# One-pass transpositions for residuals and U, U's sums on eviction, and new engine orders in a MetaFormer block

## The chip, the cores and the metric

One Trainium2 chip, one of its cores. The time is the device time in microseconds of one launch of the whole program; the kernel before has a median of 410.23 us over 3 runs (408.69 to 413.77).

## The reference

The input `x` is (8, 64, 32, 32), all float32. Four blocks follow one another, each with a residual:

```
x = x + conv0(ln_c(x))    # q, k, v by 1x1 products; softmax(k) over the 1024 pixels, softmax(q) over 16 channels
                          # of each of 8 heads; context = k v^T (16x16); out = q context; Wout, bout
t = tokens(x)             # (8, 1024, 64)
t = t + ffn0(ln_t(t))     # routing per IMAGE: mean over tokens @ Wr, softmax, capacity scale, top 2 of 8 experts;
                          # 64 -> 128 gelu -> 64 by the two experts; layer norm with gamma, beta
x = x + conv1(ln_c(x))    # 3x3 convolution 64 -> 64 with weights scaling * sign(W)
t = t + ffn1(ln_t(t))     # routing per TOKEN: softmax of logits, top 2 of 8; all 8 experts computed, weighted, summed
```

## The kernel before, in words

Everything stays in SBUF. There are two parts.

**Part one, attention**, goes over 4 pairs of images (two images of 64 channels fill 128 partitions). XC holds the pair in channels by pixels. `centre` turns tiles of 128 pixels into tokens with the channel mean subtracted (a product with the matrix `cen`), ScalarE squares, VectorE sums, GpSimd (POOL) takes the power -0.5, VectorE normalises, `xn_to_channels` turns back, `keys_values` (L530) gives keys and values. The context chain is `key_max`, `key_exp`, `kv_to_tokens` (L537), `tokens_kv`, `context` (L544), `pick_context` (Z), `context_turned` (L549), `block_diagonal` (BD), `context_out` (L559, L561), `outputs` (M). The queries go in 4 units per pair, each 2 tiles of pixels of 2 images: `queries` (L577), `query_max`, `query_exp`, `query_sum`, `qnorm` (POOL), `q_to_channels` (L589), `query_channels`. The residual of a unit opens a PSUM bank: `residual` (L605) multiplies a tile of XC by `ic`, a constant of 256 columns that holds for each image the identity and the centring matrix beside each other, so the bank gets the pixels as tokens and the centred tokens; `attend` (L618) accumulates the attention's output onto both. ScalarE squares the centred part and copies the other into T (L1267, L1270), VectorE and POOL make the token norm, `normalise2` writes U. `u_to_channels` (L632) multiplies U by IDS, an identity with a column of ones, which gives U in channels and, in column 129, its sum over the tile's tokens; `u_channels` (ScalarE, L1279) copies both into UT. After pair 3 the router (L1002 and on) sums those columns and picks two experts for each image.

**Part two** goes image by image, software pipelined: while image b goes through its 8 experts (`f_hidden` L696, `f_gelu` L1388, `f_gated` L1186, `f_output` L801), image b+1 goes through the convolution and the token router (`a_vT`, `b_conv`, `b_to_tokens`, `b_residual`, `b_centre`, `b_ss`, `b_normalise`, `b_to_channels` L759, `b_gates` L766, `b_logits`, `b_probs`, `b_first`, `b_second`, `b_weights`, `b_gates_turned` L772) and image b+2 through the image-routed layer (`a_hidden`, `a_output` L712, `a_z_turned`, `a_sum`, `a_ss0`, `a_zn`, `a_residual`, `a_centre`, `a_ss1`, `a_normalise`). The 8 x 1024 token weights GT are stored to DRAM and loaded back, each broadcast to 128 partitions (GB, 512 KB each); `f_gated` multiplies by them. The outputs of the 8 experts accumulate in a PSUM bank; `f_start` adds the weighted biases (B2X times GT, L789) and the residual (TF times the identity, L791) with `start=False` between `f_output2` and `f_output3`, in program order behind `b_gates` of the next image. `f_result` copies the bank out, which is stored.

Each engine runs one stream. The order in it is written out by hand: `ATTENTION_PLAN` for part one and `PLAN` for part two give, per engine, a cyclic list of parts; `name+2` in period p is that part for pair or image p+2. Parts named `set_` run once (where p + ahead is 0) and prepare weights: `set_conv` (L863 to L873) makes the signs of the convolution weights in place in W1stage, loaded last by the sync engine's queue, writes WC, and sums the absolute weights from a second load into W1stage that waits for the signs. A queue never looks past a waiting instruction; dependencies between engines are counting semaphores.

## Time and profile before

| | us |
|---|---|
| median of 3 runs | 410.23 |
| the profiled execution, its own time | 412.51 |
| its span, first to last instruction | 410.7 |
| TensorE busy | 344.7 (84%) |
| VectorE, ScalarE, POOL busy | 278.7, 230.0, 92.8 |
| DMA moved | 41.17 MB |

The profile is one execution. Part one runs to about 118 us, the router to 127, a start-up of part two with little overlap to about 180, six full image periods to about 357, and the last image to the end. A float32 product is two MATMUL records, a transposition one. Records of TensorE overlap in time, so what a part costs is read from its start to the next start. The granted clock of TensorE (PEclk) is 1 at 2.4 GHz and 0.5 at 1.2 GHz; a share between them is a stretch with both.

### The profile page before, as it was taken

What the parts mean: (1) busy time and instruction counts of PE and PEld (TensorE: products, weight loads), DVE (VectorE), ACT (ScalarE), POOL (GpSimd) and SP (SyncE); (2) the same over time, 40 slices, a digit from 0 to 9 for tenths busy, and PEclk for the clock granted to TensorE, in tenths of its full rate; (3) what the DMA queues carried; (4) which work ended last, traced back from release to release, by engine and by line L of the source; (5) the groups of instructions that cost most, each with busy time, mean ns of one, the idle gap of its engine ahead of it and who ended that gap; (6) DMA issues with size and microseconds to landing.
All of it is one profiled execution on the core that took longest, in us unless ns stands there. A gap on an engine that the chain in (4) does not pass through costs nothing.

```text
span 410.7 us, 5254 instructions
## 1 busy us (share of the span) xinstructions
PE 344.7 (84%) x1751; PEld 188.1 (46%) x1751; DVE 278.7 (68%) x587; ACT 230.0 (56%) x392; POOL 92.8 (23%) x77
## 2 busy tenths in 40 slices
PE   4879899998927146689999999999999999888975
PEld 4357687876922032333443443443443444344222
DVE  3486995959441524727977968868959959966662
ACT  2445466464525314555756857857857856736631
POOL 5226271643410111211112112103103103102000
PEclk9699999999975758579999999999999999999988
DMA  6941000000000000028039048057066065073092
GB/s 153 178 119 31 1 2 2 0 2 1 2 1 0 0 2 1 0 74 339 1 103 336 0 128 311 0 155 285 0 207 233 0 229 211 3 292 144 26 344 95
DMA packets 25835, 41.17 MB, mean 100 GB/s; under 512 B 15376, under 2 KB 16144, under 8 KB 25808
## 3 DMA queue, kind: packets, MB, share of 16 engines
q1 hardware_dynamic: 25808, 40.83, 30.9%
q8 instruction: 14, 0.23, 0.2%
q14 instruction: 13, 0.11, 0.1%
HBM read 38.47 MB, written 2.36 MB: 99 GB/s over the span
## 4 chain that ended last, share of the span: by engine, by line
PE 41%; DVE 25%; issue 13%; ACT 10%; POOL 5%; DMA 3%; POOLq 1%; ACTq 0%; SPq 0%; DVEq 0%
PE ps L696 9%; PE ps L742 6%; PE ps L801 5%; POOL rstdA L457 4%; PE ps L605 3%; PE ps L712 3%; DVE HB L1186 3%; PE ps L618 2%; PE ps L530 2%; PE ps L513 2%; PE ps L727 2%; DVE qsum L964 2%; ACT XC L1336 2%; ACT HB L1388 2%; DVE ssA L1092 2%
## 5 line engine op out<-in xcount | busy, mean ns | idle before, releaser
L696 PE MATMUL ps<-ET,W1B 64*128 64x512 f32 x256 | 70.4, 655 | 6.9 <-ACT HB L1388 5.3
L1186 DVE TENSOR_TENSOR HB<-HB,GB 128x1024 f32<-128x1024 f32 x44 | 53.1, 1220 | 23.9 <-DMA GB<-spread 23.8
L1388 ACT ACTIVATE HB<-ps,B1B 128x1024 f32<-128x1024 f32 x44 | 47.8, 1111 | 9.4 <-PE ps L696 5.3
L457 POOL TENSOR_TENSOR rstdA<-varA,pow_half 128x8 f32<-128x8 f32 x16 | 28.8, 1801 | 90.8 <-DVE varA L886 90.8
L801 PE MATMUL ps<-HB,W2B 128*64 128x512 f32 x176 | 45.2, 617 | 3.7 <-DVE HB L1186 3.7
L457 POOL TENSOR_TENSOR rstdB<-varB,pow_half 128x8 f32<-128x8 f32 x8 | 14.0, 1750 | 124.7 <-DVE varB L886 124.7
L696 PEld LDWEIGHTS ps<-ET,W1B 64*128 64x128 f32 x256 | 21.9, 194 | 35.8 <-issue 12.0
L457 POOL TENSOR_TENSOR rstd<-var,pow_half 128x4 f32<-128x4 f32 (+1 forms) x24 | 29.0, 1217 | 21.1 <-DVE var L886 20.8
L742 PE MATMUL ps<-VP,WC 128*128 128x512 f32 x96 | 28.4, 450 | 1.4 <-ACT VP L1356 1.4
L1186 DVE TENSOR_TENSOR XC<-XC,GB 128x1024 f32<-128x1024 f32 x20 | 24.2, 1219 | 5.9 <-DMA GB<-spread 5.9
L472 POOL TENSOR_TENSOR QS<-QS,rqsum 128x512 f32<-128x512 f32 x16 | 16.9, 1057 | 44.1 <-DVE rqsum L967 44.1
L742 PEld LDWEIGHTS ps<-VP,WC 128*128 128x128 f32 x96 | 19.3, 208 | 11.9 <-ACT VP L1356 6.6
L801 PEld LDWEIGHTS ps<-HB,W2B 128*64 128x64 f32 x176 | 11.1, 137 | 27.5 <-issue 23.6
L1388 ACT ACTIVATE XC<-ps,B1B 128x1024 f32<-128x1024 f32 x20 | 21.7, 1109 | 3.5 <-PE ps L801 2.1
L1356 ACT ACTIVATE VP<-ps 128x512 fp32r<-128x512 f32 x16 | 9.8, 612 | 23.2 <-PE ps L727 23.2
L696 PE MATMUL ps<-UT,W1S 64*128 64x512 f32 x64 | 20.4, 721 | 2.6 <-ACT B1S L1327 2.6
L801 PE MATMUL ps<-XC,W2B 128*64 128x512 f32 x80 | 21.4, 622 | 0.0
L1336 ACT ACTIVATE XC<-ps,B1S 128x1024 f32<-128x1024 f32 x16 | 17.8, 1112 | 2.8 <-PE ps L696 2.8
L1363 ACT ACTIVATE CV<-ps,CSCALE 128x512 f32<-128x512 f32 x8 | 5.5, 687 | 23.6 <-PE ps L742 23.6
L727 PE MATMUL ps<-ident_r,US 128*128 128x128 f32 x64 | 9.0, 267 | 11.5 <-DVE US L1082 9.9
L712 PE MATMUL ps<-XC,W2S 128*64 128x512 f32 x64 | 17.3, 629 | 1.3 <-ACT XC L1336 1.3
L1257 ACT ACTIVATE QT<-ps 128x512 f32<-128x512 f32 x16 | 9.8, 610 | 14.9 <-PE ps L589 14.9
(214 smaller groups left out, 666.7 us busy)
## 6 DMA issues: line engine op xcount, KB each, us to landing
GB<-spread SPq DMA_DIRECT2D x64, 512.0 KB, 7.9
out<-W1stage SPq DMA_DIRECT2D x8, 256.0 KB, 3.4
XC<-in_x SPq DMA_DIRECT2D x6, 256.0 KB, 5.7
...
```

The source lines that it names most:

```text
L457: pool.tensor_tensor(out_, var, pow_half[:, 0:n], ALU.pow).then_inc(s[rstd_sem], 1)
L472: pool.tensor_tensor(q, q, rqsum[:, n % 2, :].unsqueeze(2).broadcast_to([P, 32, KD]), ALU.mult)\
L605: ins = mm(a[:, j * 256:(j + 1) * 256], XC[:, p, t * P:(t + 1) * P], ic, start=(j == 0), stop=False, skip_group_check=True)
L696: mm(ps[:, H_BANKS[n % 2][c], :], weights[half(c), :], tokens(half(c)), start=True, stop=True).then_inc(s["h"], 1)
L712: ins = mm(ps[c * C:(c + 1) * C, A_BANK, :], W2S[:, k, :], HA[:, k, c * HALF:(c + 1) * HALF], start=(k == 0), stop=(k == 1), skip_group_ch ...
L727: ins = pe.transpose(ps[:, A_BANK, j * P:(j + 1) * P].bitcast(F32R), VS[:, 2 * j + h].rearrange("p k c -> p (k c)"), ident_r[:, :])
L742: ins = mm(ps[:, B_BANK, :], WC[:, dx, 3 - r:5 - r, :].rearrange("p k c -> p (k c)"), VP[:, par, r:r + H - 1:2, dx:dx + W], start=(r == 0 ...
L801: ins = mm(acc(b)[c * C:(c + 1) * C, :], W2B[:, e, :], HG[b][e][:, c * HALF:(c + 1) * HALF], start=(e == 0), stop=(e == E - 1), skip_group ...
L1186: tt(HG[b][e], HG[b][e], GB[:, e, :], ALU.mult).then_inc(s["f_hg"], 1)
L1257: av(QT[:, n % 2].rearrange("p r n -> p (r n)"), ps[:, QT_BANK, :], ACT.Copy).then_inc(s["qT"], 1)
L1336: av(HA[:, k, :], HID[n % 2], ACT.Gelu, bias=B1S[:, k:k + 1]).then_inc(s["gelu"], 1)
L1388: av(HG[b][e], HID[n % 2], ACT.Gelu, bias=B1B[:, e:e + 1]).then_inc(s["gelu"], 1)
```

## The change

- `residual` opens the bank with two transpositions (`is_transpose=True`, identity) and two products with `cen`, in place of two products with the 256 columns of `ic`.
- `u_to_channels` transposes; the sums over tokens come from `accum_out` of ScalarE's evictions, which are now one per image (USUM). IDS, its memset and its copy are gone.
- `f_start` becomes four transpositions of TF that open the accumulation ahead of `f_output0`; the bias products are a part of their own, `f_bias`, and `b_gates_out` waits for that.
- The lists of both plans are new, on all engines.

```diff
     vec=(
-        "query_sum2-2 query_max3-2 sum_squares1_1-1 normalise1_0-1 sum_squares2_0-2 query_sum3-2 normalise1_1-1 "
...
+        "sum_squares2_0-2 set_bo-1 query_sum3-2 normalise2_0-2 key_max-1 query_max0-1 sum_squares2_1-2 "
...
-                        ins = mm(a[:, j * 256:(j + 1) * 256], XC[:, p, t * P:(t + 1) * P], ic, start=(j == 0), stop=False,
+                        both = a[:, j * 256:(j + 1) * 256].rearrange("p (i x c) -> p i x c", i=2, x=2)
+                        mm(both[:, :, 0, :], XC[:, p, t * P:(t + 1) * P], ident, start=(j == 0), stop=False,
+                           is_transpose=True, skip_group_check=True)
+                        ins = mm(both[:, :, 1, :], XC[:, p, t * P:(t + 1) * P], cen, start=False, stop=False,
                                  skip_group_check=True)
...
-                        ins = mm(ps[:, UT_BANK, i * (P + 1):(i + 1) * (P + 1)],
-                                 U[:, 2 * p + i, UT_ * g:UT_ * g + UT_, :].rearrange("p h c -> p (h c)"), IDS[:, :],
-                                 start=True, stop=True)
+                        ins = pe.transpose(ps[:, UT_BANK, i * P:(i + 1) * P],
+                                           U[:, 2 * p + i, UT_ * g:UT_ * g + UT_, :].rearrange("p h c -> p (h c)"), ident)
...
             def f_start(b, par):
 
+                pe.wait_ge(s["b_t"], b + 1)
+                ge(pe, s["f_out"], b - 1)
                 for j in range(4):
-                    mm(acc(b)[:, j * P:(j + 1) * P], B2X[:, j, :], GT[:, par, :], start=False, stop=False,
-                       skip_group_check=True)
                     ins = mm(acc(b)[:, j * P:(j + 1) * P], TF[:, par, j].rearrange("p h c -> p (h c)"), ident,
-                             start=False, stop=False, skip_group_check=True)
+                             start=(j == 0), stop=False, is_transpose=True, skip_group_check=True)
                 ins.then_inc(s["f_start"], 1)
+
+            def f_bias(b, par):
+
+                pe.wait_ge(s["b_cwt"], b + 1)
+                for j in range(4):
+                    ins = mm(acc(b)[:, j * P:(j + 1) * P], B2X[:, j, :], GT[:, par, :], start=False, stop=False,
+                             skip_group_check=True)
+                ins.then_inc(s["f_bias"], 1)
...
-                    src = ps[:, UT_BANK, 0:2 * (P + 1)].rearrange("p (b n) -> p b n", b=2)
-                    av(UT[:, 2 * p:2 * p + 2, g, :], src, ACT.Copy).then_inc(s["uT"], 1)
+                    for i in range(2):
+                        ins = av(UT[:, 2 * p + i, g, :], ps[:, UT_BANK, i * P:(i + 1) * P], ACT.Identity,
+                                 accum_out=USUM[:, 2 * p + i, g:g + 1])
+                    ins.then_inc(s["uT"], 1)
```

**VectorE in part one, between pairs 0 and 1.** Before: block_diagonal and `query_max2` of pair 0, then `sum_squares1_0` of pair 1 (L904 with L886), and so on; `set_conv` (L863, L866) comes 17 rows behind the first L904.

```order
L940 TENSOR_TENSOR BD<-ps,K 128x128 x2
L951 TENSOR_REDUCE qmax<-ps 128x32
L955 TENSOR_TENSOR QS<-ps,qmax 128x512
L904 TENSOR_REDUCE ss<-SQ 128x8
L886 TENSOR_SCALAR var<-ss 128x8
L964 TENSOR_REDUCE qsum<-QS 128x32
L967 RECIPROCAL rqsum<-qsum 128x32
L951 TENSOR_REDUCE qmax<-ps 128x32
L955 TENSOR_TENSOR QS<-ps,qmax 128x512
```

Now (lines are moved by the change; L868 to L878 are `set_conv`, L909 is `sum_squares1`):

```order
L945 TENSOR_TENSOR BD<-ps,K 128x128 x2
L956 TENSOR_REDUCE qmax<-ps 128x32
L960 TENSOR_TENSOR QS<-ps,qmax 128x512
L868 TENSOR_SCALAR W1stage<-W1stage 128x576
L871 TENSOR_SCALAR WC<-W1stage 128x3x192
L876 TENSOR_REDUCE CSCALE<-W1stage 128x1
L878 TENSOR_SCALAR CSCALE<-CSCALE 128x1
L909 TENSOR_REDUCE ss<-SQ 128x8
L891 TENSOR_SCALAR var<-ss 128x8
L909 TENSOR_REDUCE ss<-SQ 128x8
L891 TENSOR_SCALAR var<-ss 128x8
```

`set_conv` with its two loads now stands ahead of the sums of squares of pair 1.

**TensorE in part two, an image period,** from `f_output7` on: before, then now (L696 `f_hidden`, L801 and now L807 `f_output`, L759 `b_to_channels`, L766 `b_gates`, L789 and L791 `f_start`; now L791 `f_start`, L799 `f_bias`).

```order
L801 MATMUL ps<-XC,W2B 64x512 x2
L719 MATMUL ps<-K,QS 128x128 x4
L696 MATMUL ps<-ET,W1B 128x512 x4
L801 MATMUL ps<-HB,W2B 64x512 x6
L759 MATMUL ps<-K,QS 128x128 x4
L696 MATMUL ps<-ET,W1B 128x512 x2
L766 MATMUL ps<-GW,ET 128x16 x4
L789 MATMUL ps<-GT,B2X 128x128
L791 MATMUL ps<-K,QT 128x128
```

```order
L807 MATMUL ps<-HB,W2B 64x512 x2
L719 MATMUL ps<-K,QS 128x128 x4
L807 MATMUL ps<-XC,W2B 64x512 x2
L696 MATMUL ps<-ET,W1B 128x512 x2
L807 MATMUL ps<-XC,W2B 64x512 x2
L696 MATMUL ps<-ET,W1B 128x512 x4
L759 MATMUL ps<-K,QS 128x128 x4
L799 MATMUL ps<-GT,B2X 128x128 x4
L766 MATMUL ps<-GW,ET 128x16 x4
L791 MATMUL ps<-K,QT 128x128 x4
L807 MATMUL ps<-HB,W2B 64x512 x2
L696 MATMUL ps<-ET,W1B 128x512 x4
```

Two `f_output` parts moved between the hidden parts, the bias products ahead of `b_gates`, `f_output2` behind `f_start`.

**TensorE, the last image,** from its `f_hidden5` before, and from `f_output5` of the image before on now.

```order
L696 MATMUL ps<-ET,W1B 128x512 x4
L801 MATMUL ps<-HB,W2B 64x512 x4
L801 MATMUL ps<-XC,W2B 64x512 x2
L696 MATMUL ps<-ET,W1B 128x512 x2
L789 MATMUL ps<-GT,B2X 128x128
```

```order
L807 MATMUL ps<-HB,W2B 64x512 x6
L696 MATMUL ps<-ET,W1B 128x512 x2
L807 MATMUL ps<-HB,W2B 64x512 x2
L696 MATMUL ps<-ET,W1B 128x512 x4
L799 MATMUL ps<-GT,B2X 128x128 x4
L807 MATMUL ps<-XC,W2B 64x512 x4
L807 MATMUL ps<-HB,W2B 64x512 x8
```

`f_hidden5` to `f_hidden7` stand behind `f_output0` now (the last two of each eight hidden products behind `f_output1`), and only the bias products are left between the outputs.

## Rows read from the trace of the kernel before

**Rows 1.** Stages by windows; per engine busy us (instructions), then clock, DMA, GB/s.
```profile
51.20:75.40 24.20, 22.55 (x155) 18.39 (x156) 18.54 (x42) 14.26 (x35) 11.44 (x11) 1.00 0.01 1
...
250.00:275.00 25.00, 24.25 (x120) 10.74 (x117) 21.09 (x43) 18.03 (x27) 5.29 (x3) 1.00 0.33 110
```

**Rows 2.** TensorE's timeline, a pair: start, us, engine, line, what [idle before, releaser].
```profile
85.53 1.93 PE L530 MATMUL ps<-XN,WKV 128*64 128x512 f32 x4 [0.36 <-ACT XN L1216]
...
89.69 0.60 PE L589 MATMUL ps<-K,QS 128*128 128x128 f32 x4
90.13 0.61 PE L632 MATMUL ps<-IDS,U 128*128 128x129 f32 x4
90.58 1.03 PE L577 MATMUL ps<-WQB,XN 128*128 128x256 f32 x4
91.44 1.03 PE L605 MATMUL ps<-K,XC 128*128 128x256 f32 x4
92.30 1.03 PE L577 MATMUL ps<-WQB,XN 128*128 128x256 f32 x4
...
98.48 0.40 PE L549 MATMUL ps<-K,Z 32*128 32x32 f32 x2 [0.69 <-DVE Z L934]
```

**Rows 3.** Timelines: keys_values of pairs 1 and 2; the router's first operation.
```profile
36.86 1.93 PE L530 MATMUL ps<-XN,WKV 128*64 128x512 f32 x4 [0.20 <-ACT XN L1216]
...
61.34 1.07 PE L530 MATMUL ps<-XN,WKV 128*64 128x512 f32 x2 [0.36 <-ACT XN L1216]
...
117.39 0.21 DVE L1002 TENSOR_REDUCE u<-UT 128x8 f32<-128x32 f32 x1 [1.27 <-ACT UT L1279]
```

**Rows 4.** TensorE's timeline, one image of the second part.
```profile
259.21 0.47 PE L789 MATMUL ps<-GT,B2X 128*128 128x128 f32 x2
...
261.17 1.99 PE L696 MATMUL ps<-ET,W1B 64*128 64x512 f32 x8
...
265.74 1.13 PE L696 MATMUL ps<-ET,W1B 64*128 64x512 f32 x4 [0.71 <-ACT HB L1388]
...
279.35 1.08 PE L712 MATMUL ps<-XC,W2S 128*64 128x512 f32 x4 [0.22 <-ACT XC L1336]
```

**Rows 5.** VectorE's timeline, then tile W1stage's view with its DMAs.
```profile
29.35 0.69 DVE L904 TENSOR_REDUCE ss<-SQ 128x8 f32<-128x512 f32 x1 [0.62 <-ACT SQ L1205]
...
37.20 0.75 DVE L866 TENSOR_SCALAR WC<-W1stage 128x576 fp32r<-128x576 f32 x1
40.97 0.75 DVE L871 TENSOR_REDUCE CSCALE<-W1stage 128x1 f32<-128x576 f32 x1 [3.01 <-DMA W1stage<-in_wcs]
...
L426 SPq DMA_DIRECT2D W1stage<-in_wconv x1: 444/444/444, 26.8 to 26.8; - x1
...
DMA to landing us min/median/max: 2.8/2.9/3.0
```

**Rows 6.** Windows, as in rows 1, behind two stretches with little TensorE work.
```profile
394.10:399.00 4.90, 4.88 (x14) 1.23 (x16) 4.29 (x4) 1.11 (x1) 0.00 (x0) 0.65 1.02 380
...
164.60:172.00 7.40, 6.69 (x20) 3.68 (x20) 4.80 (x12) 2.95 (x5) 1.46 (x1) 0.50 0.00 0
```

**Rows 7.** TensorE's timeline, the last image.
```profile
389.25 1.99 PE L696 MATMUL ps<-ET,W1B 64*128 64x512 f32 x8
394.12 3.17 PE L801 MATMUL ps<-HB,W2B 128*64 128x512 f32 x8 [2.88 <-DVE HB L1186]
...
402.56 3.60 PE L801 MATMUL ps<-HB,W2B 128*64 128x512 f32 x16
```

**Rows 8.** ScalarE's timeline in a pair.
```profile
92.28 0.18 ACT L1231 ACTIVATION_READ_ACCUMULATOR KV<-KV,nkmax 32x1 f32 x1
92.37 0.36 ACT L1279 ACTIVATE UT<-ps 128x258 f32<-128x258 f32 x1
```

**Rows 9.** VectorE's and ScalarE's timelines, the same image as rows 4.
```profile
258.68 1.22 DVE L1186 TENSOR_TENSOR HB<-HB,GB 128x1024 f32<-128x1024 f32 x1
...
262.63 0.63 ACT L1348 ACTIVATE XN<-XNT 128x512 f32<-128x512 f32 x1 [1.22 <-DVE XNT L1110]
```

More of the change, by code:

```diff
@@ L117 @@
     pool=(
[L118 removed]
+        "qnorm3-2 rstd2_1-2 qnorm0-1 rstd2_2-2 qnorm1-1 rstd2_3-2 rstd1_0 rstd1_1 qnorm2-1 rstd2_0-1"
     ).split(),
     pe=(
[L121 to L123 removed]
@@ L124 @@
-        "keys_values0+2 keys_values1+2 residual2+1 u_to_channels3 attend2+1 q_to_channels3+1 u_to_channels0+1 "
-        "queries0+2 residual3+1 queries1+2"
+        "queries2+1 kv_to_tokens+1 residual3 u_to_channels0 context+1 attend3 context_turned+1 q_to_channels0+1 "
+        "u_to_channels1 context_out+1 centre0+2 set_outputs+2 centre1+2 residual0+1 set_fold+2 queries3+1 "
+        "q_to_channels1+1 attend0+1 residual1+1 u_to_channels2 xn_to_channels0+2 attend1+1 xn_to_channels1+2 "
+        "keys_values0+2 keys_values1+2 q_to_channels2+1 set_second-2 queries0+2 queries1+2 residual2+1 "
@@ L126 @@
+        "q_to_channels3+1 u_to_channels3 attend2+1"
     ).split(),
     vec=(
[L128 to L131 removed]
@@ L132 @@
-        "normalise2_3-2"
+        "sum_squares2_0-2 set_bo-1 query_sum3-2 normalise2_0-2 key_max-1 query_max0-1 sum_squares2_1-2 "
+        "query_max1-1 normalise2_1-2 query_sum0-1 set_layer1-2 sum_squares2_2-2 order_rows1 key_norm-1 "
+        "pick_context-1 query_sum1-1 block_diagonal-1 sum_squares2_3-2 set_fold+2 normalise2_2-2 query_max2-1 "
+        "order_rows0+2 set_conv-1 sum_squares1_0 normalise2_3-2 sum_squares1_1 normalise1_0 query_sum2-1 "
+        "normalise1_1 query_max3-1"
     ).split(),
@@ L373, in build @@
             "b_eT", "b_et", "b_gate", "b_lg", "b_exp", "b_top", "b_cwT", "b_cwt", "b_out",
-            "h", "gelu", "f_hg", "f_start", "f_w2", "f_out", "f_stored",
+            "h", "gelu", "f_hg", "f_start", "f_bias", "f_w2", "f_out", "f_stored",
         ) + tuple(f"spread{e}" for e in range(E))}
```

58 lines of the change are left out of this document (23 added, 35 removed), and 8 rows, old and new, of the table pe.

## The prediction, made before the changed kernel ran

> **What bounds the kernel now.** I read the granted clock and the busy time by stage first, then TensorE's timeline in one attention pair and in one image of the second part, then the other engines at the places where TensorE waits, and last the input DMAs and the end of the run. The stage view [rows 1] shows TensorE busy for 22.55 of 24.20 us in an attention pair and for 24.25 of 25 us in the second part, at the full clock; VectorE is at 77% and 84%. So TensorE is the bound in both stages, but with waits in it. In a pair they stand at the chain over the key context, as 0.69 before `context_turned`, where VectorE's queue is late with Z [rows 2]. Summing the parts of one pair by their start-to-start times gives 21.2 us of work in a period of 24.48 and 24.19 us (`keys_values` at 36.86, 61.34 and 85.53, [rows 2, 3]): 3 us are waits. In the second part the period is 29.9 us, with two waits, 0.71 and 0.22 [rows 4].
>
> **Attention, the work.** A tile's transposition costs 0.11 us (four in 0.44, 89.69 to 90.13), an `u_to_channels` part 0.45 (to 90.58) with two float32 products, a residual part 0.86 (91.44 to 92.30) with two of 256 columns [rows 2]. Now the U part is two transpositions, 0.22. The residual part is two transpositions and two products of 128 columns, which cost what a product with the 129 columns of IDS costs, so 2 x 0.11 + 2 x 0.22 = 0.66. The gain is 0.20 + 0.23 per unit, 1.7 us per pair, and 21.2 becomes 19.5. A transposition inside an accumulation is in no row: its price lies between 0.11 and the 0.22 of the product that it replaces (residual part then 0.88, no gain); I take 0.11, since the existing ones stand between float32 products without a gap. On top of the rows: the Trainium skill's page "TensorE: Matmul & The Clock Gate", section "Terms", says that transpose mode is 4x faster for float32; these rows show 0.22 against 0.11, twice. By 4x a U part would cost 0.11 and the sum would be 1.8 us lower (16 parts).
>
> **Attention, the order.** In the new order `queries2`, `kv_to_tokens`, `residual3`, `u_to_channels0`, `context`, `attend3` and so on stand between the links of the context chain, and VectorE makes `pick_context` ahead of `query_sum1`. Laying the 30 parts of a pair out by their row durations, with each engine in its new order, leaves some 1.4 us of waits (0.6 before `context`, 0.3 and 0.4 at the two turns, the rest small). 19.5 + 1.5 = 21.0 us per pair. Bounds: 22.7 (old waits stay, or VectorE's 18.5 us of work couples badly) and 19.5. Pairs 1 to 2 and 2 to 3: 24.48 + 24.19 - 42.0 = **-6.7** (bounds -2 and -9).
>
> **Attention, the stall.** `set_conv` now stands on VectorE before `sum_squares1_0` of pair 1. It needs wconv, issued at 26.8 and landed 2.8 later, 29.6 [rows 5]; then two operations, 0.75 the longer, 1.2 together; then the second load into the same buffer, which waits for them: 3.01 us of idle before (that wait stood where VectorE would have waited for the keys anyway); then 0.75 + 0.15. So `sum_squares1_0` cannot start before about 34.9, against 29.35 [rows 5]. Behind it stand its second half (0.8 each), POOL's rstd, the normalisation and two groups of transpositions: `keys_values` of pair 1 starts at about 40.3, not 36.86 [rows 3]. That time hangs on a DMA, so the small changes at the start (WOUT's product between the halves of `centre`, under 1 us) are hidden by it. TensorE has work until about 34 and then nothing for some 4 us. After an idle stretch of 2.88 us near the end the granted clock was 0.65 over the next 4.9 us [rows 6, 7], so I count on the 1.2 GHz level for a few us here: +2.0 (bounds 0 and 4). Pair 1 is then late by **+5.5** (3.45 + 2.0; bounds +2.5 and +7.5, the low one if VectorE gets back what it no longer loses at 37 to 41).
>
> **Attention, the end.** From `keys_values` of pair 3 to the router's first operation it took 117.39 - 85.53 = 31.9 [rows 3]. The parts in it lose 2 us of work and about 1 us of waits: **-2.9** (bounds -1.5, -4). Against it ScalarE: one eviction per unit becomes two with a sum, and each sum brings a read of 0.18; the one eviction of 258 columns took 0.36 [rows 8]. Two of half its size with their reads lie between 0.72 (time goes with the columns) and 1.08 together (it doesn't); I take 0.8. ScalarE is busy 14.3 of 24.2 [rows 1], so this is hidden, except for the last unit, whose sum the router waits for: **+0.25** (bounds 0 and +1).
>
> **The second part, per image.** `f_start` was eight float32 products, 259.21 to 261.17, 1.96 us [rows 4]. Now four transpositions (0.5) and, as `f_bias`, four products (0.95): -0.45. `f_output0` and `f_output1` between `f_hidden` parts break two runs of equal products, +0.1 each. The wait of 0.71 before `f_hidden2` ends with ScalarE's gelu; ahead of that stand a table load and the squaring that waited 1.22 for VectorE's centring [rows 4, 9]. On VectorE `f_gated4` (1.22 us, at 258.68, [rows 9]) stood between `a_zn` and `a_residual`; now it fills the wait for POOL's rstd, in which `f_gated3` stood, and centring comes about 1.1 us earlier. TensorE arrives earlier too, so 0.3 to 0.4 of the wait remains. The 0.22 goes, since `f_gelu4` no longer stands behind `b_scale`. Per period -0.45 + 0.2 - 0.35 - 0.22 = -0.8 to -0.9: six of them **-5.3** (bounds -0.25 and -1.2 each). Fewer things wait for POOL or SP: both get the same instructions in the same sequence there. Before image 0, `a_residual` no longer stands behind `b_logits`: **-0.7**; in the last period **-0.6**.
>
> **The end.** `f_hidden5` and `f_hidden6` of the last image were done at 389.25 to 391.2, before the gates arrived; now they are queued behind `f_output0`, which waits for `f_gated0` and so for the GB load. From `f_output0` at 394.12 to the end at 406.16 TensorE is busy throughout [rows 7]. That stretch gains 1.9 of hidden parts and 0.2 for broken runs and loses 1.05 (`f_start` is done before, only `f_bias` stays): +1.05; and TensorE is idle from 389.3 on instead of 391.2, so the half level covers more of it: +1. **+2.1** (bounds 0 and +3.5).
>
> **Sum.** -6.7 + 5.5 - 2.9 + 0.25 - 5.3 - 0.7 - 0.6 + 2.1 = -8.35 on the profiled execution's 412.51 us, which is 2.3 above the median of 410.23; the change is the same for both, so **402.0 us**, -2.0%.
>
> **Rivals.**
> 1. *The stall costs little.* If TensorE's other parts fill it or the clock stays up, pair 1 is late by 2.5 only and the pairs come to 20.5: -12.5, **398 us**. For: the full clock held from 30 on with small waits. Against: the order leaves nothing that doesn't need VectorE.
> 2. *VectorE and its latencies set the pair.* Its 18.5 us of work per pair are as much as TensorE's 19.5; if the pairs keep their 3 us of waits, they gain 1.6 each instead of 3.3, and the end of the attention 1.5: -3.5, **406.5 us**. The same time comes out where transpositions in an accumulation are no faster than the product. For: the wait of 0.69 ended on VectorE [rows 2]. Against: the hand layout.
> 3. *Slower: the clock doesn't come back after the stall.* The place is TensorE from about 38 us on: from 164.6 on, after a wait, the granted clock was 0.50 for the whole of 7.4 us, with TensorE busy for 6.69 of them [rows 6]; 1.2 GHz is its lower level. Each us at the lower level costs 0.5; beyond about 16 us of it more than I have counted, the whole gain is gone. If it lasts through one more pair (26 us) it is +13: **415 us**. Against: attention parts are denser than those at 164, and the clock was full over whole pairs [rows 1]. The Trainium skill's page on TensorE, in its part on the transpose mode, says that the full clock does not engage for transposes, which do not count as busy in the same way; that rule speaks against this change. By it the 48 transpositions of a pair, 5.3 of 19.5 us, would not count; before it was 32 of them, 3.5 of 21.2 us, and the clock was full, so the trace gives it little weight.
>
> **Chances.** Forecast 0.50 (its own range 400 to 405), rival 1 0.24, rival 2 0.20, rival 3 0.06. The range, 395.5 to 408, takes in rivals 1 and 2 with most of the bounds. 2% is about what a measurement of this kernel can tell from no change: under 402.0 is half of the forecast and all of rival 1, 0.49; over 418.4 is the worst half of rival 3, 0.03; the rest, 0.48, lies within 2%.
>
> **What would show it.** VectorE's wait before the reduction of WCS stays near 3 us and moves to about 31 to 34, and `sum_squares1_0` of pair 1 starts at 34 to 35; the clock drops shortly after. `keys_values` start near 42, 63.5 and 84.5; the router's first operation near 113.5. The U transpositions come at 0.11 us each. The image period is 29.0 with one wait of 0.3 to 0.4 before `f_hidden2`. At the end some 14 us pass from `f_output0` of the last image to the last product. It is wrong if the transpositions among products are slower than 0.11, if an image period stays above 29.5 with new waits, or if pair 1 is not late.

## The result, and the profile after

The changed kernel takes 393.72 us (median of 4 runs, 393.04 to 394.83) against 411.08 (408.69 to 413.77) of the kernel before on the same chip: ratio 0.958, 95% interval 0.951 to 0.965. The forecast was 402.0 in a range of 395.5 to 408: the sign was right, and the gain is twice the one forecast. The profiled execution took 394.83, its span went from 410.7 to 393.0.

From the page of the changed kernel: span, busy time per engine, then TensorE's busy share and granted clock in 40 slices.

```profile
span 393.0 us, 5235 instructions
PE 333.8 (85%) x1719; PEld 179.1 (46%) x1719; DVE 279.6 (71%) x586; ACT 233.6 (59%) x440; POOL 93.0 (24%) x76
PE   3868999999817155889999999999999999898695
PEclk9978999999966658599999999999999999999968
```

TensorE is busy for 10.9 us less (344.7 before), ScalarE for 3.6 more (230.0 before, the sums on eviction are its work), VectorE and POOL for the same within 1 us. I cut both spans at the same parts:

| stretch | before | after | difference | forecast |
|---|---|---|---|---|
| start to `keys_values`, pair 1 | 36.86 | 40.47 | +3.6 | +5.5 |
| pairs 1 to 2 and 2 to 3 | 48.67 | 40.77 | -7.9 | -6.7 |
| pair 3 to the router's first operation | 31.86 | 28.67 | -3.2 | -2.65 |
| router to `f_hidden2` of image 0 | 56.89 | 56.03 | -0.9 | -0.7 |
| six periods, `f_hidden2` of image 0 to 6 | 181.16 | 171.26 | -9.9 | -5.3 |
| last period | 27.66 | 26.99 | -0.7 | -0.6 |
| `f_hidden2` to `f_output0`, last image | 11.02 | 9.94 | -1.1 | 0 |
| `f_output0` to the end of the span | 16.6 | 18.9 | +2.3 | +2.1 |

They add up to -17.7. Half of the error is in the image periods. Of the six periods before, the first took 31.66 and the others 29.90 each; now the first takes 28.18, four take 28.49 and the last 29.13.

TensorE's timeline of the changed kernel (start, us, what, idle before); these rows answer to [rows 2, 3], the router's to the last of rows 3:

```profile
40.47 2.01 PE L530 MATMUL ps<-XN,WKV 128*64 128x512 f32 x4
...
60.86 2.01 PE L530 MATMUL ps<-XN,WKV 128*64 128x512 f32 x4
...
81.24 2.01 PE L530 MATMUL ps<-XN,WKV 128*64 128x512 f32 x4
```
```profile
109.91 0.19 DVE L1007 TENSOR_REDUCE u<-USUM 128x8 f32<-128x32 f32 x1 [1.20 <-ACT UT L1284]
```

A transposition that opens an accumulation, and the product behind it, in a residual part; all of these starts are 0.11 and 0.22 apart, so the part costs 0.66 as I took it:

```profile
35.83 0.27 PE L606 MATMUL ps<-K,XC 128*128 128x128 f32 x1
35.94 0.39 PE L608 MATMUL ps<-K,XC 128*128 128x128 f32 x2
36.16 0.27 PE L606 MATMUL ps<-K,XC 128*128 128x128 f32 x1
36.27 0.39 PE L608 MATMUL ps<-K,XC 128*128 128x128 f32 x2
```

Windows over one pair and one image period of the changed kernel, which answer to [rows 1]:

```profile
60.86:81.24 20.38, 20.25 (x156) 16.85 (x156) 18.62 (x42) 15.01 (x47) 11.49 (x10) 1.00 0.01 2
251.09:279.58 28.49, 28.31 (x134) 12.04 (x134) 23.95 (x47) 20.74 (x31) 5.29 (x4) 1.00 0.45 158
```

TensorE is busy for all but 0.13 of a pair and 0.18 of an image period, at the full clock. Before, 24.19 held 22.55 of busy time, and an image period of 29.90 held 28.93. So its busy time fell by 2.3 per pair and by 0.62 per image, and its idle time by 1.5 per pair (1.64 to 0.13) and 0.8 per image. One image period, with the waits of [rows 4]: 0.71 has become 0.18, and before the two halves of L712, which now run as one, nothing is left of 0.22.

```profile
251.09 1.13 PE L696 MATMUL ps<-ET,W1B 64*128 64x512 f32 x4 [0.18 <-ACT HB L1395]
...
263.40 1.94 PE L712 MATMUL ps<-XC,W2S 128*64 128x512 f32 x8
```

VectorE ahead of pair 1, which answers to [rows 5]: the stall is where it was forecast, with the length that it was forecast to have.

```profile
30.35 0.75 DVE L871 TENSOR_SCALAR WC<-W1stage 128x576 fp32r<-128x576 f32 x1
34.05 0.75 DVE L876 TENSOR_REDUCE CSCALE<-W1stage 128x1 f32<-128x576 f32 x1 [2.95 <-DMA W1stage<-in_wcs]
34.84 0.15 DVE L878 TENSOR_SCALAR CSCALE<-CSCALE 128x1 f32<-128x1 f32 x1
34.91 0.68 DVE L909 TENSOR_REDUCE ss<-SQ 128x8 f32<-128x512 f32 x1
```

### The profile page after: what moved, and what is told of

It reads as the page before. It is cut to its first block, busy times and chain, and to the rows that moved or that the text cites. A ratio compares the mean times of both kernels' runs of the same rounds, so it can differ in the third digit from the quotient of the medians.

```text
span 393.0 us, 5235 instructions
## 1 busy us (share of the span) xinstructions
PE 333.8 (85%) x1719; PEld 179.1 (46%) x1719; DVE 279.6 (71%) x586; ACT 233.6 (59%) x440; POOL 93.0 (24%) x76
## 4 chain that ended last, share of the span: by engine, by line
PE 45%; DVE 17%; ACT 13%; issue 10%; SPq 6%; DMA 5%; POOL 2%; POOLq 1%; ACTq 0%; DVEq 0%
PE ps L696 14%; PE ps L807 9%; PE ps L742 5%; PE ps L712 3%; ACT HB L1395 3%; DMA GB<-spread 3%; SPq L411 2%; POOL rstdA L457 2%; DVE qsum L969 2%; ACT L1382 2%; ACT L1395 2%; PE ps L727 2%; DVE HB L1191 1%; PE ps L621 1%; ACT XN L1355 1%
## 5 line engine op out<-in xcount | busy, mean ns | idle before, releaser
L696 PE MATMUL ps<-ET,W1B 64*128 64x512 f32 x256 | 70.2, 652 | 2.4 <-ACT HB L1395 1.9
L807 PE MATMUL ps<-HB,W2B 128*64 128x512 f32 x176 | 47.5, 630 | 3.7 <-DVE HB L1191 3.7
L696 PEld LDWEIGHTS ps<-ET,W1B 64*128 64x128 f32 x256 | 21.5, 193 | 45.8 <-issue 25.2
L742 PE MATMUL ps<-VP,WC 128*128 128x512 f32 x96 | 28.4, 450 | 1.4 <-ACT VP L1363 1.4
L1395 ACT ACTIVATE XC<-ps,B1B 128x1024 f32<-128x1024 f32 x20 | 21.8, 1113 | 3.5 <-PE ps L807 2.3
L472 POOL TENSOR_TENSOR QS<-QS,rqsum 128x512 f32<-128x512 f32 x16 | 16.9, 1058 | 24.9 <-DVE rqsum L972 24.9
L696 PE MATMUL ps<-UT,W1S 64*128 64x512 f32 x64 | 19.6, 695 | 2.6 <-ACT B1S L1334 2.6
L807 PEld LDWEIGHTS ps<-HB,W2B 128*64 128x64 f32 x176 | 10.2, 138 | 24.4 <-issue 17.1
L807 PE MATMUL ps<-XC,W2B 128*64 128x512 f32 x80 | 21.1, 611 | 0.0
L577 PE MATMUL ps<-WQB,XN 128*128 128x256 f32 x64 | 16.0, 382 | 1.5 <-DVE QS L960 1.5
L621 PE MATMUL ps<-M,QT 128*128 128x128 f32 x128 | 17.2, 277 | 0.0
L727 PEld LDWEIGHTS ps<-ident_r,US 128*128 128x128 f32 x64 | 6.6, 145 | 22.8 <-DVE US L1087 11.5
```

The lines of the kernel that those rows point to most:

```text
L472: pool.tensor_tensor(q, q, rqsum[:, n % 2, :].unsqueeze(2).broadcast_to([P, 32, KD]), ALU.mult)\
L577: ins = mm(q[:, j * 256:(j + 1) * 256], XN[:, p % 2, t * P:(t + 1) * P], WQB[:, :], start=True, stop=True)
L621: ins = mm(a[:, r * P:(r + 1) * P], QT[:, n % 2, r, :], M[:, p % 2, r % 2, :], start=False, stop=(r == 3), skip_group_check=True)
L696: mm(ps[:, H_BANKS[n % 2][c], :], weights[half(c), :], tokens(half(c)), start=True, stop=True).then_inc(s["h"], 1)
L727: ins = pe.transpose(ps[:, A_BANK, j * P:(j + 1) * P].bitcast(F32R), VS[:, 2 * j + h].rearrange("p k c -> p (k c)"), ident_r[:, :])
L742: ins = mm(ps[:, B_BANK, :], WC[:, dx, 3 - r:5 - r, :].rearrange("p k c -> p (k c)"), VP[:, par, r:r + H - 1:2, dx:dx + W], start=(r == 0 ...
```

## The experiments

All are the changed kernel with the edits named. Times are medians, each batch on its own chip; the ratio is to the kernel before on the same chip (medians 411.4 for e1 to e4, 412.4 for e5 to e8, 411.6 for e9 to e12).

| | us | range | ratio, 95% interval |
|---|---|---|---|
| changed kernel | 393.7 | 393.0 to 394.8 | 0.958, 0.951 to 0.965 |
| e1 new orders, four-pass products | 399.9 | 397.3 to 402.4 | 0.974, 0.965 to 0.983 |
| e2 one pass, both old orders | 404.5 | 403.2 to 406.0 | 0.983, 0.975 to 0.991 |
| e3 old attention order | 397.7 | 397.3 to 398.5 | 0.966, 0.959 to 0.973 |
| e4 old order of part two | 403.5 | 400.4 to 404.3 | 0.980, 0.971 to 0.988 |
| e5 scale part later | 393.9 | 391.6 to 394.5 | 0.955, 0.950 to 0.960 |
| e6 `f_hidden5`, 6 before `f_output0` | 392.1 | 390.8 to 393.6 | 0.951, 0.946 to 0.956 |
| e7 filler products | 396.8 | 395.5 to 399.1 | 0.963, 0.957 to 0.969 |
| e8 e4, `f_gated4` early | 399.0 | 398.7 to 401.0 | 0.970, 0.965 to 0.975 |
| e9 old start of part one | 394.7 | 393.6 to 396.1 | 0.960, 0.955 to 0.964 |
| e10 e6 and e9 | 392.5 | 390.9 to 393.5 | 0.954, 0.950 to 0.958 |
| e11 e5, e6 and e9 | **389.0** | 386.3 to 390.4 | 0.944, 0.939 to 0.948 |
| e12 e8, `f_gelu4` early | 396.5 | 394.1 to 399.0 | 0.963, 0.958 to 0.969 |

For e1, e2 and e4 the interval takes in 0.98, so it isn't settled whether they gain more than 2%.

### Passes or orders: e1 to e4

One pass is my name for the transposition (one record, 0.11 us for 128 columns), four passes for the float32 product with the identity (two records, 0.22); how many passes TensorE makes no run shows.

e1 keeps the new orders and makes residuals, U and `f_start` ordinary float32 products (the same 128 columns):

```diff
-                           is_transpose=True, skip_group_check=True)
+                           skip_group_check=True)
...
-                        ins = pe.transpose(ps[:, UT_BANK, i * P:(i + 1) * P],
-                                           U[...], ident)
+                        ins = mm(ps[:, UT_BANK, i * P:(i + 1) * P], U[...], ident,
+                                 start=True, stop=True)
...
```

> New orders, but the residuals, U and the residual of the second part come from ordinary float32 products with the identity again (same number of parts, the parts of f_start and f_bias as in the changed kernel, sums still on eviction). Theory W (in the new orders TensorE's work binds): every product costs 0.11 us more per tile, 0.44 a unit of attention in both kinds of part together, 1.75 per pair, and 0.45 per image: pairs 22.2 instead of 20.4, images 28.95 instead of 28.5, about 404 us in all against 393.7. Theory C (chains of waits bind, the work hides in them): the pairs and periods grow by less than half of that, 398 to 399 us.

e2, e3 and e4 keep the new code and put back the old `ATTENTION_PLAN` (e3), the old `PLAN` with the two new names in it (e4), or both (e2):

```diff
...
-        "a_hidden1+2 b_to_tokens+1 a_output+2 f_output7-1 a_z_turned+2 f_output0 f_hidden5 f_output1 f_hidden6 "
-        "f_hidden7 b_to_channels+1 f_bias"
...
+        "a_vT1+1 f_output6-1 b_conv0+1 b_conv1+1 a_hidden1+2 b_to_tokens+1 a_output+2 f_output7-1 a_z_turned+2 "
+        "f_hidden5 f_hidden6 f_start f_output0 f_output1 f_output2 b_to_channels+1 f_hidden7 b_gates+1 f_bias f_hidden0+1 "
...
```

> The changed products with both old order tables (f_start stands right before f_output0, f_bias where f_start stood). Theory W: TensorE was the bound in the old orders too, so the pairs fall by 1.75 to about 22.5 and the images by 0.5 to 29.4: about 401 us. Theory C: the chains over the context and over gelu bound them, so pairs stay near 24 and images near 29.9: 408 to 410 us. With e1 it says whether work and order add up.

> The changed kernel with the old order table in the attention part only, so also without the early set_conv and without WOUT's product between the halves of centre. keys_values of pair 1 at about 36.9 instead of 40.5. Theory W: pairs near 22.5, the router's first operation at about 111.5, 395.5 us. Theory C: pairs near 24, the router's first operation at 116, 400 us.

> The changed kernel with the old order table in the second part only (f_start before f_output0, f_bias in its old place). Theory W: image period 29.4, Theory C: 29.9 since the gelu chain stands. The end gets better by 2 since f_hidden5 and 6 of the last image are done before the gates arrive. W: 397 us, C: 400 us. On the clock: the first image period of the second part fell by 3.5 us with the change. If that is the time at which the clock rises, which differs between executions, it will differ between these runs with no relation to their orders, and the products in it will take twice or once their time accordingly.

Read from their traces, the starts of `keys_values` and of `f_hidden2`:

| | pairs 1 to 2, 2 to 3 | image period |
|---|---|---|
| before | 24.48, 24.19 | 29.90 |
| one pass, old order (e3; e4) | 24.11, 22.95 | 29.98 |
| four passes, new order (e1) | 21.53, 21.98 | 28.68 |
| both (changed kernel) | 20.39, 20.38 | 28.49 |

Over the two pair intervals one pass alone is worth 1.6, the order alone 5.2, both together 7.9. In an image period one pass alone is worth nothing, the order alone 1.2, both 1.4.

Neither theory of these expectations holds everywhere. In the new order the pairs follow theory W (TensorE's work decides): the second of e1's two intervals, from 62.17 to 84.15, is 21.98 with TensorE busy for all of it, and going back to four passes costs 1.1 and 1.6 of W's 1.75. The images there follow theory C (the couplings between the engines decide): 0.2 of 0.45. In the old image order C holds: the period of e4 is 29.98.

The times lie between the theories (e1 399.9 between 404 and C's 398 to 399; e2 404.5 between 401 and 408 to 410; e3 397.7 between 395.5 and 400), but e4, at 403.5, is slower than either had it. In its trace the first image interval alone is 3.6 longer than the changed kernel's (31.75 against 28.18), which is mostly the clock (see e7). The four runs of e1 fall into two groups, 397.3 and 397.9 at a mean clock of 0.943 and 0.948, and 401.9 and 402.4 at 0.927 and 0.923; its trace is of the fastest.

One pass pays in full only once TensorE is the bound. TensorE's timeline of e4 shows what it does before that:

```profile
258.59 1.13 PE L696 MATMUL ps<-ET,W1B 64*128 64x512 f32 x4 [1.20 <-ACT HB L1395]
...
272.20 1.08 PE L712 MATMUL ps<-XC,W2S 128*64 128x512 f32 x4 [0.22 <-ACT XC L1343]
```

TensorE's busy time in the period fell from 28.93 to 28.55, and the wait before `f_hidden2` grew from 0.71 to 1.20 [rows 4]: what TensorE saved it waited for.

### What ends that wait: e8 and e12

e8 starts from e4 and moves two parts on VectorE; e12 also swaps two on ScalarE:

```diff
-        "b_residual+1 b_centre+1 f_gated1 b_ss+1 a_sum+2 f_gated2 a_ss0+2 b_normalise+1 f_gated3 a_zn+2 f_gated4 "
-        "b_logits+1 a_residual+2 a_centre+2"
+        "b_residual+1 b_centre+1 f_gated1 b_ss+1 a_sum+2 f_gated2 a_ss0+2 b_normalise+1 f_gated3 f_gated4 a_zn+2 a_residual+2 "
+        "b_logits+1 a_centre+2"
...
-        "a_hidden0+2 b_gates_out a_image0+1 a_image1+1 f_gelu3 b_scale+1 f_gelu4 a_hidden1+2 a_z_copy+2 b_square+1 "
+        "a_hidden0+2 b_gates_out a_image0+1 a_image1+1 f_gelu3 f_gelu4 b_scale+1 a_hidden1+2 a_z_copy+2 b_square+1 "
```

> The changed kernel with the old order of the second part, and in it one move on VectorE: f_gated4 and a_residual ahead of the places they had (f_gated3 f_gated4 a_zn a_residual b_logits a_centre). With the old order the period was 29.98, as long as before the change, though TensorE's work in it had become 0.4 less; the wait before f_hidden2 had grown from 0.71 to 1.20. Theory L (the old period is a loop over VectorE's centring, ScalarE's squaring and gelu): the centring comes about 1.1 earlier, the wait before f_hidden2 falls to 0.2 to 0.4, and the period to 29.0 to 29.2: seven periods times 0.9, 397 us against 403.5. Theory T (something else, such as ScalarE's order or POOL, ends that wait): the period stays at 29.9 to 30.0, 403.5 us.

> As e8_old_orders_gated4_early (399.0 us, period 29.44, waits of 0.66 and 0.22), and on ScalarE f_gelu4 ahead of b_scale. Theory L (the wait of 0.22 before the second half of a_hidden1 is b_scale's and f_gelu4's order on ScalarE, as the prediction said): the 0.22 goes, the period is 29.2 to 29.25, and the run at 397.5 us. Theory R (that wait only moves into the one before f_hidden2): the period stays at 29.4 with one wait of 0.9, 399 us.

The period fell from 29.98 to 29.43 (e8) and 29.06 (e12), the time from 403.5 to 399.0 and 396.5. TensorE's timeline of e8, then of e12:

```profile
269.22 1.08 PE L712 MATMUL ps<-XC,W2S 128*64 128x512 f32 x4 [0.23 <-ACT XC L1343]
...
285.04 1.13 PE L696 MATMUL ps<-ET,W1B 64*128 64x512 f32 x4 [0.66 <-ACT HB L1395]
```
```profile
252.48 1.13 PE L696 MATMUL ps<-ET,W1B 64*128 64x512 f32 x4 [0.72 <-ACT HB L1395]
...
281.53 1.13 PE L696 MATMUL ps<-ET,W1B 64*128 64x512 f32 x4 [0.71 <-ACT HB L1395]
```

So the loop over VectorE's centring and ScalarE's gelu that the prediction named is real: each move takes its piece off (0.55 and 0.37; the 0.22 is gone in e12). In size theory L was too hopeful for e8 (0.66 of the wait stayed, not 0.2 to 0.4) and not hopeful enough for e12 (29.06 for 29.2 to 29.25; theory R, by which the period stays at 29.4, fell). Between e12 and the changed kernel lie 0.57 per period that came with the rest of the new order; which of its moves brings them was not tried.

### The stall and the start: e5, e9, e11

In e5 the sign part of `set_conv` stays, and the part that waits for the second load becomes `set_scale`:

```diff
+            def set_scale(p, par):
                 vec.wait_ge(s["ld_conv"], 32)
...
-        "query_max1-1 normalise2_1-2 query_sum0-1 set_layer1-2 sum_squares2_2-2 order_rows1 key_norm-1 "
+        "query_max1-1 normalise2_1-2 query_sum0-1 set_scale-2 set_layer1-2 sum_squares2_2-2 order_rows1 key_norm-1 "
```

> The changed kernel, but of the weight fold of attention pair 1 only the sign part stays on VectorE where the change put it; the part that scales WCS (which waits for the second load into the weight buffer) is its own step, just ahead of set_layer1. Theory S (the stall costs what its wait is, and hardly any clock): VectorE's 2.95 of idle go from before sum_squares1_0 of pair 1, keys_values of pair 1 starts at 37.0 to 37.8 instead of 40.5, and everything after it is earlier by the same 3: 390.5 to 391 us. Theory F (the stall stands where other waits would stand): keys_values of pair 1 no earlier than 39.5, 393 us. If the pairs after it need the head start (queues that drift), the periods 1 to 2 and 2 to 3 would grow from 20.4; I expect 20.4 and 20.4.

In e9 `set_outputs` (on TensorE and ScalarE) and `set_fold` (on VectorE) go back behind the parts that they had been moved ahead of, and `order_rows1` stands ahead of `set_conv` again:

```diff
-        "u_to_channels1 context_out+1 centre0+2 set_outputs+2 centre1+2 residual0+1 set_fold+2 queries3+1 "
+        "u_to_channels1 context_out+1 centre0+2 centre1+2 residual0+1 set_fold+2 set_outputs+2 queries3+1 "
...
-        "pick_context-1 query_sum1-1 block_diagonal-1 sum_squares2_3-2 set_fold+2 normalise2_2-2 query_max2-1 "
-        "order_rows0+2 set_conv-1 ...
+        "pick_context-1 query_sum1-1 block_diagonal-1 sum_squares2_3-2 set_fold+1 normalise2_2-2 query_max2-1 "
+        "order_rows0+2 order_rows1+2 set_conv-1 ...
```

> The changed kernel with two moves of the attention order taken back: set_outputs stands behind set_fold again on TensorE (and in its old place on ScalarE), and set_fold stands behind order_rows of pair 0 on VectorE. Theory A (2.2 of the 3.6 by which keys_values of pair 1 is late come from the start: VectorE made set_fold ahead of the first rows, and TensorE WOUT's products between the two halves of centre): keys_values of pair 0 starts at 14.2 to 14.4 instead of 16.5, that of pair 1 at 38.3 instead of 40.5, and the run is at 391.5 us. Theory B (the load of WCS or another chain sets pair 1, whatever came before): keys_values of pair 0 is earlier by 2.2, that of pair 1 by under 0.7, and the run at 393 to 394.

| `keys_values` of | pair 0 | pair 1 | pair 2 | pair 3 |
|---|---|---|---|---|
| before | 14.31 | 36.86 | 61.34 | 85.53 |
| changed kernel | 16.53 | 40.47 | 60.86 | 81.24 |
| e5, no stall | 16.54 | 39.89 | 61.12 | 81.49 |
| e9, old start | 14.31 | 40.44 | 60.83 | 81.20 |
| e11, both | 15.09 | **37.32** | 58.57 | 78.94 |

Each edit alone gives little at pair 1, 0.6 and 0.0, and the times stay near those of theories F (393, measured 393.9) and B (393 to 394, measured 394.7); both together give 3.1. The 0.6 is between executions with the lower clock in different places: against e12 and e7, whose clock is at 0.50 from 28 to 34.6 as in e5 and whose pair 1 starts at 41.10 and 41.15, e5 gains 1.2. Two chains end at the same place. The load chain hangs on the sync engine's queue, whatever the others do. The two loads into W1stage in its timeline, of the changed kernel, then of e9:

```profile
26.88 0.45 SPq L426 DMA_DIRECT2D W1stage<-in_wconv  x1
31.13 0.33 SPq L426 DMA_DIRECT2D W1stage<-in_wcs  x1
```
```profile
27.02 0.45 SPq L426 DMA_DIRECT2D W1stage<-in_wconv  x1
31.11 0.33 SPq L426 DMA_DIRECT2D W1stage<-in_wcs  x1
```

So in e9 VectorE reached the stall earlier and left it at the same time as in the changed kernel:

```profile
29.84 0.46 DVE L868 TENSOR_SCALAR W1stage<-W1stage 128x576 f32<-128x576 f32 x1 [1.46 <-DMA W1stage<-in_wconv]
...
34.02 0.75 DVE L876 TENSOR_REDUCE CSCALE<-W1stage 128x1 f32<-128x576 f32 x1 [2.94 <-DMA W1stage<-in_wcs]
```

and in e5 the stall is gone and VectorE waits for ScalarE's squares instead, which wait for TensorE. That one came late from the start and worked at 1.2 GHz here (granted clock 0.50 from 28 to 34):

```profile
33.73 0.69 DVE L910 TENSOR_REDUCE ss<-SQ 128x8 f32<-128x512 f32 x1 [1.96 <-ACT SQ L1211]
```

With both gone (e11) it is ready at 31.75:

```profile
31.75 0.69 DVE L910 TENSOR_REDUCE ss<-SQ 128x8 f32<-128x512 f32 x1 [0.78 <-ACT SQ L1211]
```

In e5 and e11 pair 1 takes 21.2 instead of 20.4: the 0.9 of the scale part now stand in VectorE's queue of a steady pair (at 45.7 in e11), and TensorE waits for Z again:

```profile
49.00 0.40 PE L549 MATMUL ps<-K,Z 32*128 32x32 f32 x2 [1.11 <-DVE Z L940]
```

The traces also test what the prediction said of the clock behind the stall. In e9 TensorE is idle for the length that was forecast, and the clock is 1.00 from 30 to 44; in e6 (below), with the changed kernel's order of part one, it is idle for 2.08 before 38.82, and the clock is at 0.50 from 39.9 to 43.1, so that pair 1 starts at 41.63. TensorE's timeline of e9, then the window of e6:

```profile
38.26 0.66 PE L521 MATMUL ps<-K,XNT 128*128 128x128 f32 x4 [3.66 <-DVE XNT L917]
```
```profile
39.90:43.10 3.20, 3.20 (x11) 1.89 (x11) 2.29 (x6) 2.30 (x6) 1.78 (x2) 0.50 0.01 3
```

So the length of this one wait doesn't tell whether the clock falls. What does is open.

### The end: e6

```diff
-        "a_hidden1+2 b_to_tokens+1 a_output+2 f_output7-1 a_z_turned+2 f_output0 f_hidden5 f_output1 f_hidden6 "
+        "a_hidden1+2 b_to_tokens+1 a_output+2 f_output7-1 a_z_turned+2 f_hidden5 f_hidden6 f_output0 f_output1 "
         "f_hidden7 b_to_channels+1 f_bias"
```

> The changed kernel, but f_hidden5 and f_hidden6 stand ahead of f_output0 on TensorE, in every image. Theory E (the end of the run pays 2.3 us because these parts are queued behind a part that waits for the last gates, and TensorE is idle and then at the lower clock): in the last image the wait before f_output0 is 1.5 to 1.7 instead of 3.54, and the stretch from it to the end of the span 16.5 to 17 instead of 18.9; the image period stays 28.5 to 28.6: 391.5 us. Theory P (the order with f_output0 early is what shortens the image period): the period grows towards 29, and the run is at 394 to 397 us.

TensorE's last image, of the changed kernel (it answers to [rows 7]), then of e6:

```profile
374.13 1.98 PE L807 MATMUL ps<-HB,W2B 128*64 128x512 f32 x4 [3.54 <-DVE HB L1191]
```
```profile
374.91 1.08 PE L807 MATMUL ps<-HB,W2B 128*64 128x512 f32 x4 [1.41 <-DVE HB L1191]
```

The windows behind it, of the changed kernel, then of e6: 14 records of products in 5.80 us at half the clock, 24 in 4.82 at the full one.

```profile
374.20:380.00 5.80, 5.80 (x14) 1.07 (x14) 4.96 (x5) 1.11 (x1) 0.00 (x0) 0.50 1.03 379
```
```profile
375.00:380.00 5.00, 4.82 (x24) 1.92 (x26) 4.04 (x4) 2.23 (x2) 0.00 (x0) 1.00 1.04 375
```

From `f_output0` to the end it is now 16.9 instead of 18.9, with the period at 28.4: theory E. The whole is 1.6 us faster by the medians, with intervals of the ratios that overlap.

What the moved products cost by themselves e1 shows, which has them behind `f_output0` too and `f_start` ahead of it. TensorE waited for 3.25 there, and the clock stayed up:

```profile
379.50 1.08 PE L808 MATMUL ps<-HB,W2B 128*64 128x512 f32 x4 [3.25 <-DVE HB L1192]
```
```profile
379.50:385.00 5.50, 5.50 (x24) 1.89 (x25) 5.11 (x5) 2.33 (x3) 0.00 (x0) 1.00 1.01 395
```

From `f_output0` to the end of the last product it took 11.45 there, 14.33 in the changed kernel and 12.04 before (with some 4 us of it at the lower clock). So the loss at the end is the clock's, not the products'. That order doesn't bring it in every execution: e1 has none of it, and e9 about 3.5 us at the lower clock instead of 7 (17.7 to the end of the span, not 18.9).

### The clock: e7

```diff
+                    if b == 0 and h == 0:
+                        for _ in range(6):
+                            mm(ps[:, 2, :], ident, K[:, 0:512], start=True, stop=True)
...
+                if b == 0:
+                    for _ in range(3):
+                        mm(ps[:, 2, :], ident, K[:, 0:512], start=True, stop=True)
```

> The changed kernel plus nine float32 products whose result nobody reads: six on TensorE before the first transposition of the convolution of image 0, in its longest wait of the start-up (it was idle for over 9 us there), three before b_to_channels of image 0. Theory K (part of the 17.7 us that the changed kernel gained is the clock: f_hidden2 of image 0 to that of image 1 takes 1.77 and 1.76 longer than a period where the clock is at 1.2 GHz for some 6 us behind f_hidden2, and 0.3 to 0.4 less than one where it has risen before): the added products bring the clock up earlier, the convolution of image 0 (twelve products) takes 3.3 instead of 5.3, and f_hidden2 of image 0 comes 1 to 3 earlier: 391 to 392.5 us. Theory N (the start-up is set by the chain over ScalarE and VectorE, at either clock): f_hidden2 of image 0 moves by under 0.7, and the run is at 393 to 394.

The clock did rise: at 134 to 140 it was 1.00 (0.50 in the changed kernel, where TensorE did nothing in that stretch). But it was at 0.50 again from 141 to 147.7, so the convolution of image 0 took 4.86, not the 3.3 of theory K; the changed kernel has 5.32. e7 reached it 0.5 later than the changed kernel and left it level with it (148.46 and 148.42), so there the clock counts, and the experiment hardly tried it. The second stretch it did try: from 157 to 164 the clock was 1.00 (0.50 in the changed kernel) and the products L696 before `f_hidden2` of image 0 were done 3.5 sooner, but `f_hidden2` started at 165.79, in the changed kernel at 165.94, behind a wait of 3.93 for ScalarE. So theory N holds behind the convolution: TensorE isn't what `f_hidden2` waits for. And then the clock fell just there, and that cost what theory K says it costs elsewhere. TensorE's timeline and the window behind it, in e7:

```profile
165.79 2.08 PE L696 MATMUL ps<-ET,W1B 64*128 64x512 f32 x4 [3.93 <-ACT HB L1401]
```
```profile
165.00:171.00 6.00, 5.21 (x13) 1.93 (x15) 3.86 (x13) 4.12 (x5) 0.94 (x1) 0.50 0.00 0
```

| | lower clock behind `f_hidden2` of image 0 | to that of image 1, less the kernel's period |
|---|---|---|
| before | 5.5 | 31.66 - 29.90 = +1.8 |
| e4 | 5.5 | 31.75 - 29.98 = +1.8 |
| e7 | 5.6 | 30.33 - 28.49 = +1.8 |
| e8 | 3.0 | 30.27 - 29.43 = +0.8 |
| e2 | 3.4 | 30.95 - 29.98 = +1.0 |
| changed kernel, e3, e12 | 0 | -0.3, -0.4, -0.4 |

The interval grows by about 0.4 us per us at the lower clock. So 2.1 of the 9.9 us in the row of the six periods are the clock's and not the period's. In the traces that the table leaves out (e1, e5, e6, e9, e10, e11, all with the new order of part two) there is no lower clock behind this part either, so its absence goes with that order; e12, with nearly the old one, has none too, so it isn't proved that the order brings it.

e7 is slower as a whole. Pair 1 began 0.7 later, but so it did in e12, which has no filler products. And three of its late periods took 29.16, 29.53 and 28.87. In each of them VectorE, which multiplies by the loaded GB, waited a second time for the load; its timeline in the first of the three:

```profile
262.65 1.23 DVE L1197 TENSOR_TENSOR HB<-HB,GB 128x1024 f32<-128x1024 f32 x1 [2.60 <-DMA GB<-spread]
265.14 1.23 DVE L1197 TENSOR_TENSOR HB<-HB,GB 128x1024 f32<-128x1024 f32 x1 [1.26 <-DMA GB<-spread]
```

The changed kernel has the same wait, of 1.06, in its last period (the one of 29.13), and so have e3, e5, e6, e10 and e11 (28.82 to 29.29); e9 has none there and took 28.48. The periods of e4 and e12, with the old order, were even. That fits a new order that leaves less room for a late load, but no experiment moved the load.

### The best version: e10 and e11

e10 is e6 and e9 together, e11 also has e5's split.

> The changed kernel with the two moves of the start taken back and f_hidden5 and f_hidden6 ahead of f_output0: both of the places where the changed kernel loses against the one before. If the two are independent (392.1 us with the second alone, against 393.7): 389.5 to 390 us by Theory A, 392 by Theory B, in which the start gives nothing.

> As e10_best_guess, and with the scale part of the weight fold just ahead of set_layer1, so that VectorE's 2.95 of waiting before pair 1 goes too. With the changed kernel this part alone made keys_values of pair 1 only 0.6 earlier, in a stretch at the lower clock (27.8 to 34.8), and pair 1 then took 21.2 instead of 20.4. Theory C (the earlier start lets the clock stay up there): keys_values of pair 1 at 36 to 37 and 388.5 to 389.5 us. Theory D (pair 1 is set by its chain over VectorE's keys): within 0.7 us of e10.

e10 is no faster than e6 alone: Theory B, since its stall still ends at 33.9. e11 is at 389.0, 3.5 below e10 (390.4 at most against 390.9 at least) and 1.5% below the changed kernel by the ratios (0.944 to 0.958), with `keys_values` of pair 1 at 37.3 against 40.3. Its clock was at 0.50 from 25 to 31, so it isn't the clock that the earlier start saved, as its theory C had it: it was the second chain.

## Why the prediction was wrong, step by step

**The image period was mis-sized, and it is the largest error: "Per period -0.45 + 0.2 - 0.35 - 0.22", 29.0.** Those terms add to -0.82, six of them to -4.9 and not to the -5.3 taken. Measured is 28.49, which is -1.41 and outside the bound of -1.2 that I had given. I had 0.45 for the passes of `f_start` and 0.37 for the order (waits less the 0.2 for broken runs of products); the runs give 0.2 and 1.2 (e1). The waits fell by 0.8 (0.71 and 0.22 to 0.18), not by 0.57, and the 0.2 for broken runs doesn't show: TensorE's busy time fell by 0.62, not by 0.25. Five periods, 1.3 each (one of them waited for GB): -6.4 for a forecast of -4.4. The mechanism was right (e8, e12), with the error that I took the gain of `f_start` as one that stands by itself; e4 shows that it is worth nothing without the moves.

**The first period hid a clock term.** I counted six equal periods. The first took 31.66 before, 1.8 above the others, at 1.2 GHz; now the clock rises ahead of it: -3.5 for a forecast of -0.9. Some 1.4 of it is the period and 2.1 the clock, a term that I had put at nothing. The row for it stood in the trace, [rows 6] even shows its beginning, and I used it for a rival only.

**The pairs: -7.9 for -6.7.** The residual parts and U's at 0.66 and 0.22 were right. By e1 one pass is worth 1.4 per pair in the new order, where I had 1.7; the order is worth 2.6 (24.3 to 21.8), where I had 1.6. My hand layout kept 1.4 of waits; with work between the links of the context chain, 0.13 is left in pair 2. Two errors cancelled in part: the work of a new pair is 20.25 and not 19.5, and of the 3 us that I called waits before, the profile has 1.64. I had bounded the pair by 19.5 and 22.7, so the size was inside, on the side of rival 1, which had 20.5. (These two give -9.7 and -3.3 over two pairs, not the -9 and -2 of the text.)

**The stall: 3.45 + 2.0, measured +3.6, but not for these reasons.** The wait before the scale reduction, 2.95 at 34.05, and `sum_squares1_0` at 34.91 came as forecast, and so did 40.3 for `keys_values` (40.47). The 2.0 for the clock didn't: I expected TensorE idle for 4 us, and it waited for 1.63, since it came late and slow itself, and the clock stayed at 1.00 behind the wait. That it stayed up because the wait was short isn't shown: in e9 it stayed up behind 3.66, in e6 it fell behind 2.08. The lower clock came ahead of the stall, at 25.4 to 32, where before it was 1.00. And the start, for which I had under 1 us and hidden, was wrong in size (2.2 at `keys_values` of pair 0) and right in effect (e9). What I missed is that the two chains are nearly level: I priced the stall at 3.45, and taking it away alone gives back 0.6 to 1.2 at pair 1 (e5).

**The end of the attention and ScalarE's sums** -3.2 for -2.65. With the old order (e3) the stretch is 29.74 and with four passes (e1) 31.55, against 31.86 before and 28.67 now: one pass gives 2.1 alone and the order 0.3 alone. What the sums on eviction cost was not tried alone; a unit's two evictions with their reads take 0.62 on ScalarE (64.55 to 65.17), against 0.36 for the one before and below the 0.72 that I had as the least.

**Before image 0 and the last period** -0.9 and -0.7 for -0.7 and -0.6. The numbers agree, but the first can't be told from none: with the same order of part two this stretch took 55.2 to 56.8 in e1, e3, e5, e6, e9, e10 and e11, against 56.89 before. And the last period is shortest with the old order (26.80 in e4, 26.99 here), so it isn't the moves that shortened it.

**The end: +2.3 for +2.1**, right in size and partly by luck. I had +1.05 for the moved products and +1 for the clock. e6 shows that the place of `f_hidden5` and `f_hidden6` matters, but by e1 the products themselves cost nothing at the full clock; the loss is the clock's. Ahead of it stands -1.1 that no step had: in the profiled execution of before the store of the last GT took 2.85 from issue to the issue of the loads behind it, against 1.8 for the images before it. The rows of the sync engine's queue in the kernel before, then in the changed one:

```profile
385.60 0.45 SPq L435 DMA_DIRECT2D spread<-GT  x1
388.45 1.75 SPq L439 DMA_DIRECT2D GB<-spread  x4
```
```profile
366.69 0.45 SPq L435 DMA_DIRECT2D spread<-GT  x1
368.48 1.75 SPq L439 DMA_DIRECT2D GB<-spread  x4
```

It was 1.8 for the last image in all thirteen other traces, so this 1.1 belongs to one execution, not to the change.

**The rivals.** Rival 1 (398) was the nearest, still 4 us short: its pairs at 20.5 are right, and the clock stayed up, but pair 1 was late by more than its 2.5. Rival 2 (VectorE sets the pair) fell: TensorE is busy for 20.25 of 20.38. Rival 3 fell: from 33 us to the end of pair 3 the clock was 1.00. The Trainium skill's page "TensorE: Matmul & The Clock Gate", in its part on the transpose mode, has it that the full clock does not engage for transposes. The trace of this case doesn't agree where they stand among products: the pair above holds 48 of them and ran at 1.00. A stretch of transposes alone is in no run.

Nearly all the errors go the same way, and a sum of eight such terms left the range.
